# Cross-attention and a 4-bit feed-forward on one Trainium2 core: first keys and values by plain products, x ahead of most values, decoding moved by half a group

## The reference

```python
# B=8 batches of L=128 rows, D=512, H=32 heads of DH=128
h  = layernorm(x)
q  = (rmsnorm(h) * ln_weight) @ w_q.T          # split in 32 heads
k, v = ctx @ w_k.T, ctx @ w_v.T
s  = softmax(where(mask, q @ k.T + position_bias, -inf))
x  = x + h + (s @ v) @ w_out.T
W  = (NF4_CODE[w_codes] * absmax per block of 64)   # 16 codes, 4 bits
n  = layernorm(x)
return x + n @ W.T + 2 * (n @ W_a @ W_b)
```

## Time and profile before

| | before |
|---|---|
| runs | 858.46, 859.65, 859.83 us, median 859.65 |
| profiled execution | 858.53 us, of which the profile's span is 856.7 |
| PE busy | 829.1 us (97%), 4760 matmuls |
| DVE, ACT, POOL busy | 442.4, 452.4, 547.0 us |
| chain that ended last | PE 86%, DVE 5%, POOL 3%, ACT 2%, DMA 2% |
| PE's granted clock | 0.9 of full speed or more in all of 40 slices but one at 0.8 |

### The profile page before, as it was taken

How to read it: one execution, slowest core, us unless ns; L and a number is a source line. 1 busy time by engine, 2 the same in 40 slices (tenths; PEclk the granted TensorE clock), 3 DMA queues, 4 the chain that set the end, 5 groups by cost and what they waited for, 6 DMA issues and landing times.

```text
span 856.7 us, 15962 instructions
## 1 busy us (share of the span) xinstructions
PE 829.1 (97%) x4760; PEld 726.2 (85%) x4760; DVE 442.4 (52%) x768; ACT 452.4 (53%) x1314; POOL 547.0 (64%) x569
## 2 busy tenths in 40 slices
PE   7897999999999999999999999999999999999978
PEld 4786888998889888998889888998889888898756
DVE  5964556245553456345552555346552564446663
ACT  5666756354644657264644657355543657356422
POOL 1722777757676676757676677757777576848730
PEclk9998999999999999999999999999999999999999
DMA  8032313113131212213132222213132132212002
GB/s 324 23 96 65 115 41 96 57 65 95 44 109 70 88 40 90 60 60 96 44 96 88 61 67 89 61 55 96 43 96 80 45 96 89 61 41 57 25 25 87
DMA packets 51159, 65.01 MB, mean 76 GB/s; under 512 B 11008, under 2 KB 37312, under 8 KB 50112
## 3 DMA queue, kind: packets, MB, share of 16 engines
q1 hardware_dynamic: 50896, 64.53, 24.2%
q10 hardware_dynamic: 240, 0.20, 0.1%
HBM read 44.24 MB, written 4.19 MB: 57 GB/s over the span
## 4 chain that ended last, share of the span: by engine, by line
PE 86%; DVE 5%; POOL 3%; ACT 2%; DMA 2%; issue 1%; SPq 1%; ACTq 0%; POOLq 0%; DVEq 0%
PE w_ps L1216 42%; PE o_ps L1216 32%; PE s_ps L1259 6%; PE s_ps L1253 6%; POOL picked L556 1%; SPq L338 1%; POOL level L559 1%; DMA codes<-mask_dram 1%; ACT p_blocks L661 1%; DVE ctx_lo L904 1%; DVE stats L910 1%; PE w_ps L1274 0%; DVE attn_lo L904 0%; ACT resid L725 0%; DMA wv_raw<-ffn_dram 0%
## 5 line engine op out<-in xcount | busy, mean ns | idle before, releaser
L494 POOL TENSOR_TENSOR p<-pos_raw,mask_add 128x1024 f32<-128x1024 f32 x32 | 69.8, 2181 | 114.9 <-ACT p_blocks L661 114.9
L556 POOL TENSOR_SCALAR picked<-codes 128x256 f32<-128x256 int32 x112 | 121.9, 1088 | 19.4 <-POOL level L559 16.0
L661 ACT ACTIVATE p_blocks<-p,neg_max 128x128 f32<-128x128 f32 x248 | 96.1, 389 | 50.5 <-DVE neg_max L1009 43.6
L559 POOL TENSOR_TENSOR level<-level,picked 128x256 f32<-128x256 f32 x112 | 89.5, 799 | 20.6 <-POOL picked L556 20.6
L466 POOL TENSOR_TENSOR ring_lo<-k_raw,ring_hi 128x256 fp32r<-128x256 f32 x105 | 76.3, 739 | 34.6 <-ACT ring_hi L612 32.2
L612 ACT ACTIVATE ring_hi<-k_raw 128x256 fp32r<-128x256 f32 x105 | 38.7, 414 | 103.3 <-POOL k_raw L456 103.3
L1031 DVE TENSOR_TENSOR resid<-o_ps,resid 128x512 f32<-128x512 f32 x102 | 69.0, 687 | 46.5 <-PE o_ps L1216 46.4
L1216 PE MATMUL w_ps<-ctx_hi,ring_hi 128*128 128x512 f32 x210 | 85.4, 407 | 3.4 <-ACT v L612 3.4
L1216 PE MATMUL w_ps<-ctx_hi,ring_lo 128*128 128x512 f32 x210 | 82.6, 393 | 0.0
L1216 PE MATMUL w_ps<-ctx_lo,ring_hi 128*128 128x512 f32 x210 | 82.3, 392 | 0.0
L612 ACT ACTIVATE p_blocks<-p_blocks,row_scale 128x128 f32<-128x128 f32 x248 | 77.2, 391 | 1.1 <-DVE row_scale L1016 1.1
(11 more groups left out here) (221 smaller groups left out, 2326.0 us busy)
## 6 DMA issues: line engine op xcount, KB each, us to landing
pT<-p_blocks SPq DMA_DIRECT2D x496, 32.0 KB, 1.8
k_raw<-k_dram SPq DMA_DIRECT2D x16, 512.0 KB, 3.3
wv_raw<-wv_dram SPq DMA_DIRECT2D x8, 1024.0 KB, 4.8
q_raw<-q_dram SPq DMA_DIRECT2D x32, 256.0 KB, 2.9
wo_raw<-wo_dram SPq DMA_DIRECT2D x32, 256.0 KB, 4.0
resid<-x_dram SPq DMA_DIRECT2D x2, 1024.0 KB, 12.6
pos_raw<-pos_dram SPq DMA_DIRECT2D x32, 64.0 KB, 3.9
out_dram<-resid SPq DMA_DIRECT2D x8, 256.0 KB, 2.0
```

The costliest lines, as they stand in the source:

```text
L494: pool.tensor_tensor(p[:, :, :], pos, mask_add[:, :, :], ALU.add).then_inc(bias_done, 1)
L556: then(pool.tensor_scalar((level if code == 0 else picked)[:, :], codes[:, :], float(code), NF4[code], match, ALU.mult))
L559: then(pool.tensor_tensor(level[:, :], level[:, :], picked[:, :], ALU.add))
L661: e = act.activation(out(b), p[:, b, :].rearrange("p (k c) -> p k c", c=Q), ACT.Exp, bias=neg_max[:, b:b + 1], accum_out=prob_sum[:, b:b + 1])
```

## The change

The first pair's keys and the first group's values are made by plain products (8 block products, `first_keys` and `first_values`, one output tile at a time), so their weight sums are gone, and the context sums are formed later, after x is staged. The four context blocks, the key weights and then x are loaded first, the value weights behind them. PE turns the halves of x between the first value tiles; five of eight value tiles come after the scores of head 0. DVE instead of ACT scales the residual, behind head 0's softmax. Decoding starts before the loop (parts 0 and 1 of slice 0), so that in the loop heads 1 and 2 do parts 2 and 3 of this group's slice, heads 3 and 4 parts 0 and 1 of the next one's; the slice is stored and the next codes are loaded after head 2. The parts are cut anew. Within the loop nothing else is changed.

```diff
-PARTS = ((0, 1, 2, 3, 4), (5, 6, 8, 9), (10, 11), (12, 13, 14, 15))
-PART_STEP = (0, 9, 17, 21)
+PARTS = ((0, 1, 2, 3), (4, 5, 6, 8, 9, 10), (11, 12, 13, 14), (15,))
+PART_STEP = (0, 7, 19, 27)
...
+            sp.dma_start(wa, wa_d).then_inc(lora_loaded, 16)
+            sp.dma_start(wb, wb_d).then_inc(lora_loaded, 16)
             load_k(0)
-            for block_at in (BLOCK_A, BLOCK_C, BLOCK_D):
+            for block_at in range(4):
                 sp.dma_start(ctx_raw[block_at], ctx_d[block_at]).then_inc(ctx_loaded[block_at], 16)
-            sp.dma_start(wv_raw[:, :, :], wv_d[0]).then_inc(wv_loaded, 16)
             for hf in range(2):
                 sp.dma_start(resid[:, hf * HB:(hf + 1) * HB, :],
                              x_d[hf * HB:(hf + 1) * HB].rearrange("b t d -> t b d")).then_inc(x_loaded[hf], 16)
-            sp.dma_start(ctx_raw[BLOCK_B], ctx_d[BLOCK_B]).then_inc(ctx_loaded[BLOCK_B], 16)
+            sp.dma_start(wv_raw[:, :, :], wv_d[0]).then_inc(wv_loaded, 16)
+            sp.dma_start(codes[:, :], mask_d).then_inc(mask_loaded, 16)
+            load_q(0)
...
-            sp.wait_ge(lora_stored, 16 * C)
-            load_q(0)
-            sp.wait_ge(k_lo_done, PRODUCTS)
-            load_k(1)
             sp.wait_ge(q_lo_done, 1)
             load_q(1)
+            sp.wait_ge(lora_stored, 16 * C)
+            load_k(1)
...
-                        if j == G:
+                        if j == 2:
                             store_ffn(g)
                             load_codes(g + 1)
...
-            make_bias(0)
-            split_v(0, 5)
-            split_v(0, 6)
-            start_of_pair(1, 1)
-            pool.wait_ge(exp_done, 2)
-            pool.wait_ge(pos_loaded[1], 16)
-            make_bias(1)
-            go_on_pair(1, 1)
...
-                    for part in (((0,), (1, 2, 3), ())[j - 1] if last else (j - 1,)):
-                        decode(g, part)
+                    if j <= 2:
+                        decode(g, 1 + j)
+                    elif not last:
+                        decode(g + 1, j - 3)
...
+            decode(0, 0)
+            pool.wait_ge(mask_done, 2)
+            pool.wait_ge(pos_loaded[0], 16)
+            pool.wait_ge(ctx_lo_done, 6)
+            make_bias(0)
+            decode(0, 1)
+            pool.wait_ge(exp_done, 2)
+            pool.wait_ge(pos_loaded[1], 16)
+            make_bias(1)
+            start_of_pair(1, 1)
+            go_on_pair(1, 1)
...
+            act.wait_ge(k_loaded, 16)
+            copy(first_hi, k_raw[:, :, :]).then_inc(k_hi_done, PRODUCTS)
+            for n in range(4):
+                split_first(n, block_hi[n], ctx_raw[n])
+            act.wait_ge(k_lo_done, PRODUCTS)
+            for c in range(C):
+                lora_copy(c)
+            copy_first_keys(0, 1, 0)
+            copy_first_keys(1, 0, 0)
+            for half_at in range(2):
+                split_first_values(half_at)
+            copy_first_keys(2, 1, 1)
             stage_x(0)
+            copy_first_keys(3, 0, 1)
             stage_x(1)
             split_q(0)
+            copy_first_values(0)
+            split_first(4, ctx_hi[:, 2, :, :], ctx_raw[BLOCK_A])
+            split_first(5, ctx_hi[:, 4, :, :], ctx_raw[BLOCK_B])
             act.wait_ge(lnw_loaded, 16)
             xn_high(0)
+            copy_first_values(1)
+            split_first(6, ctx_hi[:, 3, :, :], ctx_raw[BLOCK_C])
+            split_first(7, ctx_hi[:, 1, :, :], ctx_raw[BLOCK_D])
             xn_high(1)
+            copy_first_values(2)
...
+            act.wait_ge(ctx_lo_done, 5)
             for hf in range(2):
                 drain_q(0, hf, first_queries[hf])
             split_q(1)
+            for hf in range(2):
+                exps(0, hf, by_blocks)
+            for hf in range(2):
+                normalise(0, hf, by_blocks)
+            for b in range(3, 6):
+                copy_first_values(b)
+            act.wait_ge(lora_stored, 16 * C)
+            copy_first_values(6)
+            copy_first_values(7)
             for p_at in range(2):
                 split_k(1, p_at, key_slot(1, p_at))
+            drain_q(1, 0, next_queries[0])
             for p_at in (2, 3):
                 split_k(1, p_at, key_slot(1, p_at))
+            drain_q(1, 1, next_queries[1])
...
+            dve.wait_ge(k_hi_done, PRODUCTS)
+            lo(first_lo, k_raw[:, :, :], first_hi).then_inc(k_lo_done, PRODUCTS)
+            for n in range(4):
+                split_first(n, block_lo[n], ctx_raw[n], block_hi[n])
             dve.wait_ge(x_loaded[0], 16)
             for b in range(HB):
                 tile_stats(b, 2 * b)
             ask_layer_power(0)
             dve.wait_ge(x_loaded[1], 16)
+            tile_stats(HB, 2 * HB)
             ask_rms_power(0)
+            for half_at in range(2):
+                split_first_values(half_at)
+            for b in (HB + 1, HB + 2):
                 tile_stats(b, 2 * b)
             stage_factors(0)
+            tile_stats(HB + 3, 2 * HB + 6)
             ask_layer_power(1)
+            dve.wait_ge(mask_loaded, 16)
+            dve.tensor_scalar(mask_add[:, :, :], mask_raw, 1.0, -MASKED, ALU.subtract, ALU.mult).then_inc(mask_done, 1)
+            ask_rms_power(1)
             dve.tensor_reduce(row_valid[:, :], mask_raw, AX.X, ALU.max).then_inc(mask_done, 1)
             stage_factors(1)
             split_q(0)
+            context_sum(1, BLOCK_C, BLOCK_D, ALU.add)
+            context_sum(3, BLOCK_A, BLOCK_C)
+            dve.wait_ge(ctx_sums, 1)
+            context_sum(2, BLOCK_D, BLOCK_A)
+            dve.wait_ge(ctx_sums, 3)
+            context_sum(4, BLOCK_B, BLOCK_A)
             x_norm(dve.tensor_scalar(ln_scale[:, :], rstd[:, :], 1.0, None, ALU.add), False)
+            x_norm(dve.scalar_tensor_tensor(ln_shift[:, :], mean_var[:, :, 0], -1.0, rstd[:, :], ALU.mult, ALU.mult))
+            split_first(4, ctx_lo[:, 2, :, :], ctx_raw[BLOCK_A], ctx_hi[:, 2, :, :])
+            split_first(5, ctx_lo[:, 4, :, :], ctx_raw[BLOCK_B], ctx_hi[:, 4, :, :])
...
+                if hf == 0:
+                    split_first(6, ctx_lo[:, 3, :, :], ctx_raw[BLOCK_C], ctx_hi[:, 3, :, :])
+                    split_first(7, ctx_lo[:, 1, :, :], ctx_raw[BLOCK_D], ctx_hi[:, 1, :, :])
...
+            for b in range(B):
+                dve.wait_ge(staged, b + 1)
+                dve.tensor_scalar(resid[:, b, :], resid[:, b, :], ln_scale[:, b:b + 1], ln_shift[:, b:b + 1],
+                                  ALU.mult, ALU.add).then_inc(hidden_done, 1)
...
+            def first_keys(head, hf, last=False):
+                pairs = [((first_hi[:, 2 * c + head, s * DH:(s + 1) * DH], first_lo[:, 2 * c + head, s * DH:(s + 1) * DH]),
+                          (block_hi[2 * hf + c][:, s, :], block_lo[2 * hf + c][:, s, :]))
+                         for c in range(2) for s in range(2)]
...
+            def first_values(b):
+                hf = b // HB
+                at = slice(b % HB * L, (b % HB + 1) * L)
+                if b >= 3:
+                    pe.wait_ge(values_copied, b - 2)
+                pairs = [((block_hi[2 * hf + c][:, s, at], block_lo[2 * hf + c][:, s, at]),
+                          (first_value_hi[c][:, :, s, :], first_value_lo[c][:, :, s, :]))
+                         for c in range(2) for s in range(2)]
...
+            pe.wait_ge(k_lo_done, PRODUCTS)
             pe.wait_ge(ctx_lo_done, 2)
+            first_keys(1, 0)
+            first_keys(0, 0)
             pe.wait_ge(ctx_lo_done, 4)
+            first_keys(1, 1)
             pe.wait_ge(lora_copied, C)
+            first_keys(0, 1, True)
+            pe.wait_ge(wv_lo_done, PRODUCTS)
+            first_values(0)
+            turn_x(0)
+            first_values(1)
+            turn_x(1)
+            first_values(2)
             for hf in range(2):
                 pe.wait_ge(xn_lo_done, C * (hf + 1))
                 queries(0, hf, first_queries[hf])
             scores(0, 1)
+            for b in range(3, B):
+                first_values(b)
+            for hf in range(2):
+                queries(1, hf, next_queries[hf])
+            pe.wait_ge(ctx_lo_done, SPLITS)
```

More of the change, by code:

```diff
@@ L704, in lora_copy, with copy_first_keys, copy_first_values @@
                      scale=LORA_SCALE).then_inc(lora_copied, 1)
+            def copy_first_keys(n, head, hf):
+                act.wait_ge(keys_done, n + 1)
+                copy(kT[:, head, half(hf)], first_key_banks[head][hf]).then_inc(keys_copied, 1)
+            def copy_first_values(b):
+                act.wait_ge(values_done, b + 1)
+                copy(v[:, b, :], first_value_banks[b % 3]).then_inc(values_copied, 1)
             def stage_x(hf):
                 act.wait_ge(norm_done, hf + 1)
-                act.wait_ge(ctx_lo_done, (2, 4)[hf])
+                if hf == 1:
+                    act.wait_ge(wv_lo_done, PRODUCTS)
                 for b in halves(hf):
-                    at = resid[:, b, :].rearrange("p (c n) -> p c n", c=C)
```

(19 more changed lines are left out.)

285 lines of the change are left out of this document (67 added, 218 removed).

## The result

The changed kernel takes 867.33 us (median of 4 runs, 866.21 to 867.86), the kernel before 859.06 in the same comparison (858.31 to 859.83): a ratio of 1.0094 with a 95% interval of 1.0081 to 1.0107. It is slower by 8.3 us; the prediction said 863.9, with a range of 858.5 to 869.0.

A forecast was written before the change was run, and what follows sets the result against it. PE was taken to bound the kernel, never waiting inside the loop. Terms +13.3 - 6.6 - 2.0 = +4.7 us on the profiled 858.53 gave 863.2, plus 0.6 for the median: 863.9, range 858.5 to 869.0.

The forecast's parts named there:

- Loop: Seven groups: PE waits about 1.9 us each for POOL's low parts of the value weights; +13.3 us (bounds 7 to 17).
- Lateness: How late POOL becomes per group at the value weights' low parts in the fourth head: 3.6 us (bounds 2.54 and 4.1).
- the third head's spill: Part of POOL's delay: third head's seven decoding steps outlast the idle time before the fourth head's bias by 0.75 us.
- the fourth head's twelve steps: Part of POOL's delay: six code pairs in the fourth head instead of four pairs and two single steps, 2.54 us more.
- overlaps: Part of POOL's delay: an addition of POOL falls under DVE's low part of the queries, taken as 0.3 us.
- 1.55: Margin in us by which POOL's low part for value product 2 precedes PE's need, after a hand-over of 0.15.
- Tail: Program end: last slice decoded earlier, so DVE's low part comes 6.7 us sooner; -6.6 us (bounds -4.1 and -7.5).
- Start: Before the loop: second query product ends earlier, less the cost of eight residual scalings on DVE; -2.0 us (bounds -5 and +3).
- the third head absorbs its steps: Rival, loop: nothing spills or overlaps between POOL's decoding and the fourth head's bias; -1.6 us in all, 857.5; chance 0.11.
- the waits in each group lower the clock: Rival, loop: slow matmuls behind each group's wait, 1.85 us a time, seven times 13 us, 877; chance 0.06.
- the start loses: Rival, start: x is needed before the values that were its cover; +3 instead of -2, 868.9; chance 0.09.
- the full lock: Rival, loop: of POOL and a two-input DVE step, the second waits for the whole first; +2.8 us, 866.7; chance 0.10.

The follow-up runs named there:

- experiment 1: The changed kernel with decoding parts cut evenly: 5, 8, 10 and 8 steps in heads 3, 4, 1 and 2 (change: 7, 12, 8, 4); 855.53 us.
- experiment 2: The changed kernel with only the third head's decoding longer than before: 7, 10, 6 and 8 steps in heads 3, 4, 1 and 2; 855.58 us, one run.
- experiment 3: The changed kernel with only the fourth head's decoding longer than before: 3, 12, 8 and 8 steps in heads 3, 4, 1 and 2; 859.88 us, one run.
- experiment 6: The kernel of experiment 1 with DVE's eight residual scalings moved ahead of the third head's query split; 851.21 us.
- experiment 7: Also `e7_best1`: the kernel of experiment 6, with POOL's bias of head 1 also waiting until DVE has scaled head 0's row sums; 849.84 us.
- experiment 4: The changed kernel with DVE's eight residual scalings moved ahead of the third head's query split; 863.34 us.
- experiment 5: The kernel of experiment 1 with the last slice finished late again: in the last group, 22 POOL steps in head 2, four of them unused; 861.98 us.
- experiment 8: The kernel of experiment 7 with x rounded earlier in the start: on ACT both halves before the context splits, on DVE the first before the sums; 844.82 us.

## Why the prediction was right, and where it was off

The direction and the main mechanism were right; the time was 3.4 us short by the medians (867.33 against 863.9), and 4.4 on the profiled executions (+9.1 against +4.7).

- **Loop: +13.3 forecast, +12.5 measured.** Lateness 3.6 forecast, 3.34 measured. In parts: the third head's spill 0.75, measured 0.68 (443.12 - 456.30 = -13.18 from product 0, against 435.06 - 448.92 = -13.86); the fourth head's twelve steps 2.54 and overlaps 0.3, measured 13.12 for 10.40, or 2.72. From lateness less 1.55 to the group's length it came out to 0.01 us, and experiments 1 to 3 show that this is the mechanism. The exactness is in part luck: POOL's low part for product 2 ends at 462.41 + 1.28 = 463.69 and PE starts at 463.75, so the hand-over is some 0.05 us and not the 0.15 that was taken, and the margin is 1.65. The other 0.1 comes behind the wait, where product 4 starts 5.85 us after product 2 (469.60) instead of 5.76 (460.44 before).
- **Tail: -6.6 forecast, -6.8 measured in the forecast place.** The move of DVE's low part was 6.8 us (7.37 less 0.60) where 6.7 was forecast, and the stretch of PE that hangs on it went from 19.42 to 12.64 us, also 6.8. In it are the wait of 4.1, a gap of 1.51 that is now 0.57, and the slow products between: before, the stretch behind the wait ran at a granted clock of 0.81, and now at 1.00. These are PE's stretches between the output products and the feed-forward, before (from the end of the wait) and after; the columns are us, busy, granted clock, DMA share, GB/s:

```profile
820.30:828.60 8.30, 6.74 (x27) 0.81 0.00 0
```

```profile
825.00:837.60 12.60, 12.08 (x56) 1.00 0.00 1
```

From there to the end nothing changed (28.10 and 28.16). The other 1.1 us of the -7.8 lies ahead of this stretch and belongs to the last scores, below.

- **Start: -2.0 forecast, +2.0 measured. This is the step that failed**, most of it in one term: "0.35 each and 2.8 in all; the bias ends 0.6 after PE wants it". The place and the kind of the cost were named; the size was wrong twice. The eight scalings took 4.16 us and not 2.8: they start 0.46 us apart where 0.35 was taken (3.71 us for the eight where POOL leaves them alone, in experiments 6 and 7), and POOL held up the first by 0.42. And the wait they made, 2.42 us instead of 0.6, brought the lower clock with it, which I had priced only as a rival for the loop: 3.31 us for the sixteen products that take 1.8 to 1.95 at full clock. Experiment 4 shows that this block is worth 3.8 us, 3.2 more than it was given. The price had no row in fp32; the measured 0.46 lies midway between the 0.35 that was taken and the 0.6 of the two-input row. The Trainium skill (VectorE: DVE Perf Modes, The perf-mode tier table) puts such a one-input fp32 step at twice the rate of a two-input one; this case's rows say 0.54 against 0.68 us, so it was no ground for the lower price. The rest of the miss is small terms. The second query product was forecast to end at 55.0 and ends at 55.65 (56.90 before), so this part gained 1.25 us and not 1.9. And from the end of head 0's attention to the first value products, where the sum had nothing, it takes 71.69 us where it took 70.60 before; in experiment 4, with no slow products there, it is 71.94, with waits of 0.2 for ACT's `kT` and 0.5 for DVE's `attn_lo` in it.
- **Last scores: +2.4 at the mark, not forecast; 1.3 in the end.** PE waits 2.0 us instead of 1.3 for the last head's `attn_lo`, since the block moves land late (ACT's softmax of that head waits 2.48 us for them), and the sixteen products then ran at a granted clock of 0.54. In the executions of the experiments this wait lay between 1.8 and 2.4 us and the products took 2.05 to 3.48 us, so part of it varies from run to run. Why the moves land later there stays open; it is not how long SP issues them (11.16 us here and 10.27 in experiment 1, with waits of 2.02 and 1.99 behind). The slow products cost less than their length: from the start of these scores to the last output products it is 19.68 to 19.70 us in the four kernels that had them slow (the change, experiments 4, 5 and 6) and 19.07 to 19.13 in the six others, so 0.6. Those six have a wait of 0.8 us for ACT's `p` in this stretch, and the four do not. So 1.1 of the 2.4 comes back before the output products.
- **The rivals.** That the third head absorbs its steps: refuted by the change itself, true of its mechanism below the margin (experiment 2). That the waits in each group lower the clock: refuted; at waits of 0.82 and 0.46 us the stretch behind has a granted clock of 1.00. That the start loses: true, but by the eight steps and not by PE's idle stretches, which experiment 8 shows to be worth 5 us of their own, a cost that my sum had paid inside the -2.0 without calling it one. Of the full lock, below: the mechanism was there, but the sum already held part of its price.

## What to carry to other kernels

An engine that is 60% busy can still set the time: measure the margin of each hand-over to the engine that bounds, from two timelines, and compare every moved step with it; here 1.55 us decided in three kernels. When work is shifted over a loop's boundary, cut it anew so that no stretch ahead of a tight hand-over grows. And put a block of steps that nobody waits for into an idle stretch of its queue (12 us stood open one instruction earlier), never ahead of what the bounding engine needs next.

## What the runs showed of the hardware that was not expected

- **A whole-step block between DVE and POOL.** A two-input DVE step of 4 columns took 2.00 us instead of 0.16 when POOL's two-input step had begun 0.17 us earlier, in experiments 1, 2, 3, 5 and 6, each time until POOL's step ended. The kernel before has the same pair in its start, so its trace could have settled what the prediction left open:

```profile
66.63 2.14 POOL L494 TENSOR_TENSOR p<-pos_raw,mask_add 128x1024 f32<-128x1024 f32 x1 [1.08 <-ACT p_blocks L661]
```

```profile
66.79 1.99 DVE L1016 TENSOR_TENSOR row_scale<-recip,row_valid 128x4 f32<-128x4 f32 x1
```

With the order turned round by one semaphore (experiment 7) it took 0.16. A one-input step is held up too: the first of the eight scalings took 0.96 us in the change, and 2.14 in experiment 8, where POOL's bias had begun 0.29 us ahead of it, each time until 0.28 us after POOL's step. The 1.13 us by which my overlap was priced fit the same: DVE's step gives way to its next at 389.66 in that head, and POOL's ends at 389.21 + 1.13 = 390.34, or 0.68 later, close to a whole addition of 0.73. The Trainium skill (SBUF — State Buffer, Who interferes with whom) says that the port pair which DVE shares with POOL is an exclusive lock, and that issue order decides who blocks; the traces agree. So the rival of a full lock named the right mechanism, at the wrong price. Part of the price stood in the sum already: the 8.44 us of the earlier trace rows hold the addition of 1.13 and this one,

```profile
386.60 1.17 POOL L559 TENSOR_TENSOR level<-level,picked 128x256 f32<-128x256 f32 x1 [0.18 <-POOL picked L556]
```

and in the change's third head the same two take 1.23 and 1.13, where one alone takes 0.73. For this head the 0.3 was counted a second time. What came beyond the sum's other terms was 0.06 us in the third head (8.50, forecast 8.44) and 0.18 in the fourth (13.12 - 10.40 - 2.54), where one comparison beside DVE's low part of the queries took 1.28 us instead of 1.07.
- **The lower clock is not a fixed price of a wait.** Waits of 1.99 and 2.17 us ahead of the last scores left the sixteen products at 2.05 us, waits of 2.02 and 2.19 us made them 3.67 and 3.48. Two stretches of PE at these products, of the change and of `e7_best1`; the third number is the granted clock.

```profile
805.30:809.00 3.70, 3.69 (x17) 0.54 0.21 53
```

```profile
788.00:790.10 2.10, 2.06 (x17) 1.00 0.22 57
```

0.54 is near the lower of the two levels (1.2 GHz of 2.4) for nearly the whole stretch. Behind a wait of some 2 us these products may or may not take 1.4 to 1.6 us more, so it should stand in a range and not in a sum; of that, 0.6 us is left where the last output products begin (above).
